# A four-layer cross-attention model on one core: a re-ordered lead-in of its second layer, third-layer queries by tiles, an attention stored in three parts, and two experts added from PSUM

## The reference

```
x = x + tanh(g_xattn[0]) * L0_xattn(layernorm(x), ctx, ctx, mask)   # linear attention, 16 heads, features relu(LN(.)) + 1e-6
x = x + tanh(g_ffn[0])   * L0_ffn(layernorm(x))                     # ternary weights, int8-like rows, silu(gate) * up
x = x + tanh(g_xattn[1]) * L1_xattn(layernorm(x), ctx, ctx)         # window of 65 keys, rotary, 16 heads: keys 0 to 55 only
x = x + tanh(g_ffn[1])   * L1_ffn(layernorm(x))                     # 16 experts, top 2, and 2 shared
x = x + tanh(g_xattn[2]) * L2_xattn(ctx, layernorm(x), mask)        # 8 heads of 64, l2-normed q and k, context and latents as keys
x = x + tanh(g_ffn[2])   * L2_ffn(layernorm(x))                     # ternary weights, gelu
x = x + tanh(g_xattn[3]) * L3_xattn(ctx, ctx, layernorm(x))         # 16 heads of 8, softmax over 1500 keys
x = x + tanh(g_ffn[3])   * L3_ffn(layernorm(x))                     # 8 experts, top 2
```

## Time and profile before

| | |
|---|---|
| runs of this kernel | 844.57, 846.31, 850.4 us (median 846.31) |
| profiled execution | 849.31 us, span 847.5 us |
| busy: TensorE, VectorE, ScalarE, GpSimd | 754.1, 608.8, 411.9, 338.3 us |
| moved | 88.35 MB, mean 104 GB/s |
| granted clock of TensorE, mean | 0.94 |

### The profile page before, as it was taken

The page is one execution under the profiler, slowest core; times in us unless marked ns, Lnnn a source line. Parts: engine busy times, 40 slices in busy tenths (PEclk is TensorE's granted clock), DMA queues, the critical chain, the costliest instruction groups (busy, mean ns, idle before and its releaser), DMA issues.

```text
span 847.5 us, 15714 instructions
## 1 busy us (share of the span) xinstructions
PE 754.1 (89%) x5632; PEld 496.9 (59%) x5632; DVE 608.8 (72%) x1264; ACT 411.9 (49%) x675; POOL 338.3 (40%) x271
## 2 busy tenths in 40 slices
PE   4699999996778988997899999997799998998997
PEld 3577777785445475653455555563346665655575
DVE  4889999997887755565655556658789997525653
ACT  2476666673465524424445444421127775834331
POOL 0665555553523601540587787732241211100111
PEclk9899999997998968999999999998959999998999
DMA  7256766532425530206022233006746677000320
GB/s 202 94 193 216 244 211 202 162 122 84 55 85 183 159 108 0 84 29 173 1 77 76 78 110 106 8 14 100 111 84 132 123 147 157 3 2 26 98 89 23
DMA packets 50582, 88.35 MB, mean 104 GB/s; under 512 B 17374, under 2 KB 34974, under 8 KB 50166
## 3 DMA queue, kind: packets, MB, share of 16 engines
q1 hardware_dynamic: 50518, 87.49, 38.4%
HBM read 61.97 MB, written 25.51 MB: 103 GB/s over the span
## 4 chain that ended last, share of the span: by engine, by line
PE 46%; DVE 38%; ACT 5%; POOL 4%; issue 4%; DMA 2%; SPq 0%; DVEq 0%; POOLq 0%; ACTq 0%
DVE arena L2360 9%; PE ps L1111 8%; DVE arena L1759 8%; PE ps L1101 6%; DVE rn L1914 4%; PE ps L1279 3%; DVE arena L1963 3%; PE ps L1044 3%; PE ps L1289 3%; DVE arena L1942 2%; PE ps L1216 2%; PE ps L1205 2%; DVE arena L1922 2%; POOL arena L1696 2%; PE ps L1057 1%
## 5 line engine op out<-in xcount | busy, mean ns | idle before, releaser
L1759 DVE TENSOR_TENSOR arena<-ps,arena 128x448 f32<-128x448 f32 (+7 forms) x138 | 83.4, 628 | 58.4 <-ACT arena L1564 20.6
L2360 DVE TENSOR_REDUCE arena<-ps 112x1 f32<-112x500 f32 x192 | 114.4, 668 | 9.0 <-PE ps L1188 9.0
L1696 POOL TENSOR_TENSOR arena<-arena 125x448 f32<-125x448 f32 x96 | 109.5, 1141 | 24.2 <-ACT arena L1509 21.2
L1111 PE MATMUL ps<-arena 125*128 125x448 f32 (+1 forms) x208 | 97.1, 548 | 1.4 <-ACT arena L1509 1.0
L1540 ACT ACTIVATE arena<-ps 125x896 f32<-125x896 f32 x96 | 87.3, 917 | 22.4 <-PE ps L1205 22.4
L1509 ACT ACTIVATE arena<-arena,kbias 125x448 f32<-125x448 f32 x96 | 63.7, 668 | 65.3 <-DVE arena L1759 46.3
L1759 DVE TENSOR_TENSOR arena<-ps,rn 125x448 f32<-125x448 f32 x96 | 59.3, 618 | 47.7 <-PE ps L1101 43.3
L1101 PE MATMUL ps<-arena 128*125 128x448 f16 (+3 forms) x312 | 77.8, 359 | 3.0 <-DVEq L1770 3.0
L1101 PEld LDWEIGHTS ps<-arena 128*125 128x125 f16 (+1 forms) x312 | 40.9, 135 | 57.2 <-issue 42.3
L803 PE MATMUL ps<-w_k2h,arena 128*125 128x512 f16 x288 | 67.8, 388 | 6.9 <-ACT arena L1345 5.2
L1673 POOL TENSOR_TENSOR arena<-arena 112x512 f32<-112x512 f32 x24 | 30.4, 1267 | 90.4 <-DVE arena L1759 90.3
(11 more groups left out here) (307 smaller groups left out, 1469.8 us busy)
## 6 DMA issues: line engine op xcount, KB each, us to landing
arena<-in_ctxT SPq DMA_DIRECT2D x8, 750.0 KB, 7.9
d_cln<-arena SPq DMA_DIRECT2D x8, 750.0 KB
d_clnT<-arena SPq DMA_DIRECT2D x8, 750.0 KB
d_k<-arena SPq DMA_DIRECT2D x24, 250.0 KB
d_v<-arena SPq DMA_DIRECT2D x24, 250.0 KB
arena<-d_clnT SPq DMA_DIRECT2D x8, 750.0 KB
arena<-in_ctx SPq DMA_DIRECT2D x8, 672.0 KB
arena<-d_cln SPq DMA_DIRECT2D x8, 672.0 KB
```

The source lines that it names most:

```text
L1111: pe.matmul(ps[0:D, 4 + 2 * p, 0:N], cln_s[p][0:rows, t, :], pexp[(t + p) % 2][0:rows], start=(t == 0), stop=(t == KT)).then_inc(l2_pv, 1)
L1696: ins = pool.tensor_tensor(psum2[p][0:rows], psum2[p][0:rows], pexp[(t + p) % 2][0:rows], ALU.add)
L1759: return dve.tensor_tensor(out, a, b, op)
L2360: dve.tensor_reduce(mx3[bn % 2][:, u % 2, u % 8 // 2, u // 8:u // 8 + 1], ps[0:TT, max_bank_of(bn, u), 0:500], AX.X, ALU.max).then_inc(l3_ ...
```

## The change

- Batch 0 makes three units (its three thirds), the others one each as before: `turn_units`. So units 0 to 9 are done in the pass, 10 to 23 in the lead-in, one or two fewer at most places, and unit 23 stands after the second attention. Only units 20 to 23 are loaded after the norms.
- In the last batch ScalarE makes `rhs0` from the context, and VectorE multiplies norm and gain in one operation for each of 12 tiles, in two halves; TensorE begins its sums with the first.
- The turned sums are copied in halves, by VectorE and ScalarE; the padding of the second attention is written by ScalarE instead of GpSimd.
- The rounding of quantised weights moves behind the first attention. That is stored in three parts, each when it is ready, and read back in two.
- Three of the six last key norms, and their maximum, move behind the quantising of the first network.
- The last two experts are added to `x` straight from PSUM, scaled by the gate. (These two are the shared ones, whose weight is 1.)
- The joined matrices `m2` and the scaling of `w_kT2` move from before the experts to behind them; third-layer queries go by tiles of 112 tokens and without the zero padding, by halves of the rows; twelve more `keep_clock` matmuls stand before the scores.

```diff
+UNITS = [(0, 0), (0, 1), (0, 2)] + [(b, 0) for b in range(1, B)] + \
+    [(b, third) for b in (7, 6, 1, 2, 3, 4, 5) for third in (1, 2)]
+IN_TURNS, RELOADED = B + 2, B + 6
...
+            for k in range(3):
+                some = slice(3 * k, min(3 * k + 3, B))
+                sp.wait_ge(l0_att, k + 1)
+                sp.dma_start(d_att[some].rearrange("b h n e -> n (b h) e"),
+                             at0[:, some].rearrange("n b (h e) -> n (b h) e", h=H16)).then_inc(l0_st[k], 16)
...
-            for u in range(8, 13):
+            for u in range(IN_TURNS, 16):
                 store_later(u)
             sp.wait_ge(rn_sq, 1)
-            for u in range(18, 24):
+            for u in range(20, 24):
                 load_later(u)
...
+                if not more:
+                    act.wait_ge(l0_w, b + 1)
+                    act.wait_ge(acc_full, b + 1)
+                    for j in range(KT):
+                        ins = act.activation(rhs0[:, j, 0:D], c_in[p][:, j, :], ACT.Identity, scale=sm[:, 11, j:j + 1])
+                    ins.then_inc(l0_rhs, 1)
...
+                    for half in range(2):
+                        some = slice(6 * half, 6 * half + 6)
+                        for j in range(6 * half, 6 * half + 6):
+                            ins = dve.scalar_tensor_tensor(kn[:, j, :], kraw[:, j, :], sm[:, 9, 2 * j:2 * j + 1],
+                                                           spread("L0_g", KP, 1)[:, 0, :], ALU.mult, ALU.mult)
+                        ch.link(ins)
+                        ch.link(tt(kn[:, some], kn[:, some], spread("L0_b", KP, 6), ALU.add))
+                        dve.tensor_scalar(kpr[:, some], kn[:, some], 0.0, 1e-6, ALU.max, ALU.add).then_inc(l0_kp, 1)
...
-            l2_norms(B, 0, range(KT // 2, KT))
-            dve.wait_ge(sq_used, KT * B + SQ)
+            l2_norms(B, 0, range(KT // 2, 9))
...
             quantise(big2, big3, hq, ((4, 2),), ffn=0)
+            l2_norms(B, 0, range(9, KT))
+            dve.wait_ge(sq_used, KT * B + SQ)
...
-            weigh(E1 - 2, 0, wts[:, :, E1 - 2:E1 - 1], 0)
-            weigh_last(5, E1 - 1, wts[:, :, E1 - 1:E1], 0)
+            dve.wait_ge(ex_acc, E1)
+            residual(5, y2)
+            for e in range(E1 - 2, E1):
+                dve.wait_ge(ex_dn, e + 1)
+                residual(5, ps[0:TT, 6 + e % 2, :].rearrange("p (t n) -> p t n", t=NT))
...
-            for c in range(4):
-                for t in range(NT):
-                    mm = pe.transpose(ps[0:D, c, TT * t:TT * t + TT], big[:, t, D * c:D * c + D],
+            for t in range(NT):
+                op.next()
+                for c in range(4):
+                    mm = pe.transpose(ps[0:D, t, TT * c:TT * c + TT], big[:, t, D * c:D * c + D],
                                       ident[0:TT, 0:TT])
-            mm.then_inc(product, 1)
+                mm.then_inc(product, 1)
             op.next()
             for h in range(H8):
-                mm = pe.matmul(ps[0:D, (4 + h) % 8, 0:N], w_kT2[:, h // 2, :], qT2[:, h, :], start=True, stop=True)
+                rows = slice(64 * (h % 2), 64 * (h % 2) + 64)
+                pe.matmul(ps[0:D, h, 0:N], w_kT2[rows, h // 2, :], qT2[rows, h // 2, :], start=True, stop=True)\
+                    .then_inc(product, 1)
+            op.next()
+            keep_clock(12, 2)
```

More of the change, by code:

```diff
@@ L188, in a_uses @@
 def a_uses(b):
-    return 20 * b - 12 if b else 0
+    return 20 * b - 8 if b else 0
 def build(nc, io, out):
@@ L922, in quantised_ffn @@
                 if n == 0:
-                    later(13, 14)
+                    later(14, 15, 16)
                 else:
@@ L949, in _ @@
             quantised_ffn(0, 0, 2, 2)
-            later(15, 16, 17, 18)
+            later(17, 18)
             op.next()
@@ L1018, in _ @@
             by_tokens(xT2, w_l1[:, 3, :], 0)
-            pe.wait_ge(ld_m, 5 * 16)
-            for h in range(H8):
-                r, c = 64 * (h % 2), h // 2
-                mm = pe.matmul(ps[0:D, 6 + h % 2, D * c:D * c + D], w_vT2[r:r + 64, c, :], w_o2[r:r + 64, c, :],
-                               start=True, stop=True)
-            mm.then_inc(l2_m, 1)
-            keep_clock(14, 3)
+            later(23)
+            keep_clock(6, 3)
             op.next()
@@ L1068, in _ @@
                 expert1(E1 // (2 * G1) - 1, s, more=s < 2 * G1 - 1)
-            keep_clock(26, 3)
+            pe.wait_ge(ld_m, 5 * 16)
+            pe.wait_ge(ex_w, E1 + 2)
+            for h in range(H8):
+                r, c = 64 * (h % 2), h // 2
+                mm = pe.matmul(ps[0:D, 6 + h % 2, D * c:D * c + D], w_vT2[r:r + 64, c, :], w_o2[r:r + 64, c, :],
+                               start=True, stop=True)
+            mm.then_inc(l2_m, 1)
+            keep_clock(14, 3)
             op.next()
@@ L1461, in _ @@
             heads_joined1(NT - 1)
-            act.wait_ge(l2_m, 1)
-            act.copy(m2.rearrange("p (c r) n -> p r c n", r=2),
-                     ps[0:D, 6:8, :].rearrange("p r (c n) -> p r c n", c=4)).then_inc(l2_m, 1)
+            later(23)
             def silu1(e, p):
@@ L2246, in _ @@
             signal(lat_ready)
-            product_in.next(4)
+            dve.wait_ge(ld_m, 5 * 16)
+            ch.link(tt(qk_col[:, 0:1], qk_col[:, 0:1], qk_col[:, 1:2], ALU.mult))
+            ch.step(dve.tensor_scalar(w_kT2, w_kT2, qk_col[:, 0:1], 8.0, ALU.mult, ALU.mult))
             for t in range(NT):
@@ L2308, in batch2 @@
                     if first and t == 6:
-                        rounded_weights(slice(3, 5))
-                    if first and t == 8:
                         quantised_weights(slice(3, 5))
```

253 lines of the change are left out of this document (136 added, 117 removed).

## The result

| | before | changed |
|---|---|---|
| median | 848.0 us (4 runs, 844.57 to 850.4) | 838.75 us (4 runs, 836.14 to 839.38) |
| profiled execution, its span | 849.31, 847.5 us | 838.38, 836.6 us |

The account below looks back on a forecast made before the run. TensorE and VectorE were taken to carry the chain in turns, transfers only 2%. Eight terms, from a 2.2 us loss to a 6.9 us gain, summed to 20.5 us, giving 828 us; range 817 to 840.

Parts of the forecast that it names:

- (a): Third layer's setup: half clock slows the head products, with the last batch at its worst as well: 838 us; chance 0.14.
- (b): Second layer: late loads of units 20 to 22 make moved units come back elsewhere, term 6 gives nothing: 837; chance 0.12.
- term 5: Second layer's lead-in, fewer units ahead of transposes and norms moved: gain 5.65 us (2.0, 0.35 and 3.3).
- terms 2 and 3: Last batch, ScalarE making the right-hand side: gain 1.7 us; joining, `kvt` copied in halves: 2.85 us more.
- term 8: Third layer's setup, from its layernorm to first scores: gain 6.9 us, bounds 4 to 8.
- term 7: Experts: 0.6 us from the router's chain and 2.2 us at the end, where experts are added straight from PSUM.
- Term 1: Batch 0, two more units: ScalarE's third unit waits for a `late_k` buffer, a loss of 2.2 us.
- Term 4: First attention stored in three parts: transfer hidden but for 1.1 us, gain 0, bounds -0.5 and +1.1 us.
- term 3: Joining: `kvt` copied in halves on two engines, remainders and rounding moved behind; gain 2.85 us, bounds 1.5 and 3.5.
- Term 6: Second attention, one unit fewer between scores and output: gain 2.8 us, bounds 0 to 2.9.
- (c): Slower: the same load queue blocked so long that unit 20 comes 25 us late: 854 us; chance 0.04.
- (d): Every gain but the experts' tail and the setup goes to a second wait: 842 us; chance 0.06.

Follow-up runs that it names:

- Quiet z: GpSimd starts the remainders that follow a layernorm only when VectorE has written z, against the changed kernel: 836.3 us, ratio 0.9831 to the kernel before.
- the repetition: The changed kernel measured once more, unchanged, in the rounds of the combinations: 836.84 us, ratio 0.9849 to the kernel before.

## Why the prediction was right or wrong

- **The sum** is half, and the range held by the room that I had left for rivals (a) and (b), not by the forecast's bounds of 12 to 26 us; so that it held is partly luck. What failed are two waits that I had put at nothing (the copy of `k1T`, the clock ahead of the second attention) and term 5's size, 7.1 us together; terms 2 and 3, 2.5 us better than forecast, hid part of it. Of the rest, 3.4 us were missing in term 8, most of them by a chance fall of the clock, 1.0 in term 7 and 0.9 behind.
- **Term 1**: right, -2.0 for -2.2, by the buffer and GpSimd's order, and 1.9 of it free to avoid.
- **Terms 2 and 3**: right in kind, 7.1 us for 4.55. The sums ran at full clock; in the joining TensorE's value products (2.05 us) did too, and VectorE had GpSimd out of its way: the three scalings of the weights took 1.28 us instead of 2.83.
- **Term 4**, -2.3 for 0. The stores themselves were worth 0, as forecast. No run bears out the 4 us more that an estimate there puts on three stores: the last load went out 2.8 us sooner with three than with one. What failed is a sentence of term 3, that ScalarE's zeroing "ends near 211, in time for unit 10". It did end there (211.8); but I had followed only unit 10 behind it, not the copy of `k1T` that is queued behind that, for which TensorE waits 2.38 us. Moving it gave 2.2 of the 2.3 us back.
- **Term 5** was 2.1 too large: 1.1 for 1.4 us up to the copy of the first network's transposes, 0.4 for 0.95 up to the down projection, 2.0 for 3.3 behind it. Units count only until VectorE is the later one: from the down projection to the copy are 8.2 us, of which 2.88 are z beside GpSimd, a duration that I didn't take up into the 6.9. Quiet z gives 1.66 back there. The clock in the projection didn't stay up either, but VectorE, which takes its products without a wait, lost nothing by that.
- **Missing altogether**: the clock in the second attention's lead-in, 2.65 us. I counted each unit moved away as TensorE's time saved; here it was also what kept TensorE busy. My rival (a) had the right mechanism in the wrong place. In the head products, where I had put it, the clock was 1.00.
- **Term 6** right (2.9 for 2.8). **Term 7** 1.0 too large: less than 0.1 of the 0.6 ahead of the experts arrived, where VectorE now waits 1.94 us instead of 1.13 for the reciprocal root, which GpSimd does behind a remainder (with quiet z it is 1.13 again); the tail gave 1.8 for 2.2, and the two times given for it, 377.4 and 375.4, make only 2.0.
- **Term 8**, 3.5 for 6.9 in the profiled execution, but 23.87 us against a forecast of 23.75 in the repetition, there 6.5 for 6.9 up to the first product with values. The steps were right. What I didn't weigh is that a fixed number of clock matmuls ahead of a critical step lasts twice as long at half clock; 1.3 and 1.9 us went so. Of the 0.9 from the scores' clock 0.5 came.
- **Behind**: 0.9 us, which I had left out as a mishap of up to 0.5. The second quantising operation (1.24 us) stands in the loop, which lost 0.2 us, and the fourth layer's lead-in lost 0.4; the rest stays open.

Rivals (b), (c) and (d) are refuted: TensorE never waits for `in_ctxT` in the second layer, and the lead-ins did gain.

## What to carry to other kernels

Before work is moved out of a stretch in which TensorE waits for others, ask what keeps its clock there; fill the waits with matmuls that nobody reads, started as soon as a bank is free, and, which no run here tried, few enough to end before the operand comes even at 1.2 GHz. When a step is given to an idle engine, list everything queued behind it, not only the next instruction, and ask what it waits for. Place another engine's work beside VectorE's critical steps only where it doesn't take the same ports.

## What the runs showed of the hardware

- The same program keeps 2.4 GHz in a stretch of one execution and drops to 1.2 in another: 12 matmuls of 512 columns took 2.76 or 4.4 us. Between two executions of the changed kernel such chance made 2.9 us in the third layer's setup (26.75 and 23.87).
- VectorE's four scaling operations of 112x128 took 1.11 us alone and 1.87 to 2.88 beside GpSimd's remainders; a rounding of 112x512 took 0.43 and 1.18.
- Eight head products over 64 rows each took 3.28 us, where the same eight over 128 zero-padded rows had taken 6.28, both at a granted clock of 1.00: half the time, as if two products on different rows of the array ran at once. The Trainium skill ("TensorE: Matmul & The Clock Gate", Part 3: Packing small matmuls) says the same of small matmuls placed on distinct row groups.
